# Choosing PSUM banks by a replay on another set of engine intervals, in an attention and feed-forward block

## The reference

```python
q = _rope(q, positions)
k = _rope(k, positions)
scores = jnp.einsum('bhqd,bhkd->bhqk', q, k) / jnp.sqrt(jnp.float32(dk))
scores = jnp.where(causal[None, None, :, :], scores, -jnp.inf)
attn = jax.nn.softmax(scores, axis=-1)
out = jnp.einsum('bhqk,bhkd->bhqd', attn, v)
...
x = _layernorm(x + _L0_attn_ref(x, L0_attn_W_qkv, L0_attn_W_o), axis=-1)
x = _layernorm(x + _L0_ffn_ref(x, L0_ffn_kernel, L0_ffn_bias, L0_ffn_a, L0_ffn_b), axis=-1)
```

## Time and profile before

| | |
|---|---|
| median of 3 runs | 437.37 us (437.16 to 437.58) |
| profiled execution | 437.25 us, span 435.5 us |
| busy, share of the span | PE 95%, PE weight loads 47%, DVE 86%, ACT 72%, POOL 26% |
| mean granted TensorE clock | 0.985 |
| chain that ended last | PE 78%, DVE 15%, ACT 4% |

### The profile page before, as it was taken

The page is one execution under the profiler, slowest core; times in us unless marked ns, Lnnn a source line. Parts: engine busy times, 40 slices in busy tenths (PEclk is TensorE's granted clock), DMA queues, the critical chain, the costliest instruction groups (busy, mean ns, idle before and its releaser), DMA issues.

```text
span 435.5 us, 8512 instructions
## 1 busy us (share of the span) xinstructions
PE 412.0 (95%) x3250; PEld 202.5 (47%) x3250; DVE 374.5 (86%) x487; ACT 313.5 (72%) x552; POOL 114.6 (26%) x184
## 2 busy tenths in 40 slices
PE   5999799999999999999999999999999999999992
PEld 2556444354335453465453544444354354436651
DVE  2878889999999989998899999999989977657586
ACT  2454765785776877686877797978786888898761
POOL 8879610202212111212011213003003001205534
PEclk9999889999999999999999999999999999999997
DMA  7522322200000000022200022200000000000011
GB/s 236 187 99 78 133 65 69 74 25 3 0 2 3 2 2 4 2 70 60 75 3 2 6 81 62 59 2 2 2 2 2 2 2 2 3 2 3 3 50 49
DMA packets 12200, 16.57 MB, mean 38 GB/s; under 512 B 2444, under 2 KB 7324, under 8 KB 12160
## 3 DMA queue, kind: packets, MB, share of 16 engines
q1 hardware_dynamic: 11072, 15.75, 11.6%
q0 software_dynamic: 1088, 0.28, 0.4%
HBM read 10.37 MB, written 5.24 MB: 36 GB/s over the span
## 4 chain that ended last, share of the span: by engine, by line
PE 78%; DVE 15%; ACT 4%; issue 2%; DMA 1%; SPq 0%; DVEq 0%; ACTq 0%
PE ps L1296 28%; PE ps L1280 19%; PE ps L1227 17%; DVE pmax L1038 13%; PE ps L1195 3%; ACT probs L961 3%; PE ps L1305 2%; PE ps L1241 2%; PE ps L1237 1%; PE ps L1211 1%; PE ps L1324 1%; PE ps L1201 1%; DMA x_sb<-in_L_attn_x_dram 1%; PE ps L1251 1%; PE ps L1328 1%
## 5 line engine op out<-in xcount | busy, mean ns | idle before, releaser
L1038 DVE TENSOR_REDUCE pmax<-ps 128x2 f32<-128x1024 f32 (+3 forms) x273 | 318.4, 1214 | 35.3 <-PE ps L1227 20.0
L961 ACT ACTIVATE probs<-ps 128x512 f32<-128x512 f32 (+4 forms) x485 | 282.1, 655 | 81.9 <-PE ps L1280 80.8
L1280 PE MATMUL ps<-qS,kS 64*128 64x512 f32 (+3 forms) x664 | 149.9, 404 | 2.8 <-DVE pmax L1038 2.3
L1296 PE MATMUL ps<-probs,vP 128*9 128x512 f32 (+3 forms) x1328 | 146.4, 520 | 0.2
L1227 PE MATMUL ps<-kS,qS 64*128 64x512 f32 (+3 forms) x640 | 137.1, 418 | 6.6 <-DVE pmax L1038 2.3
L1280 PEld LDWEIGHTS ps<-qS,kS 64*128 64x128 f32 x664 | 78.4, 187 | 81.0 <-ACT probs L961 45.6
L1227 PEld LDWEIGHTS ps<-kS,qS 64*128 64x128 f32 x640 | 64.9, 186 | 68.5 <-DVE pmax L1038 29.1
L868 POOL TENSOR_SCALAR_AFFINE_SELECT probs<-probs 128x512 f32<-128x512 f32 x64 | 40.4, 635 | 123.3 <-ACT probs L961 123.2
L877 POOL DMA_DIRECT2D qS<-mrows x34 | 19.6, 578 | 163.5 <-DVE mrows L1058 163.5
L1296 PEld LDWEIGHTS ps<-probs,vP 128*9 128x9 f32 x1328 | 21.1, 88 | 39.2 <-issue 26.8
L1241 PEld LDWEIGHTS ps<-causal_x,ident_x 64*128 64x128 f32 x188 | 17.9, 186 | 0.0
(11 more groups left out here) (120 smaller groups left out, 188.5 us busy)
## 6 DMA issues: line engine op xcount, KB each, us to landing
qS<-q_parts SPq DMA_DIRECT2D x52, 64.0 KB
kS<-k_parts SPq DMA_DIRECT2D x52, 64.0 KB
cs<-rope_tables_dram SPq DMA_DIRECT2D x4, 512.0 KB, 6.7
q_parts<-qp SPq DMA_DIRECT2D x4, 512.0 KB, 2.8
k_parts<-kp SPq DMA_DIRECT2D x4, 512.0 KB, 2.8
x_sb<-in_L_attn_x_dram SPq DMA_DIRECT2D x4, 256.0 KB, 5.8
out_dram<-rot SPq DMA_DIRECT2D x2, 256.0 KB, 2.4
qS<-mrows POOLq DMA_DIRECT2D x30, 8.0 KB, 1.8
```

Source lines behind the costliest of these rows:

```text
L961: nc.scalar.activation(probs[:, J % PRING, heads[0]:heads[-1] + 1:3 - len(banks), lo:hi], src, ACT.Exp, scale=float(DK) ** -0.5).then_inc( ...
L1038: nc.vector.tensor_reduce(dst, src, AX.X, ALU.max).then_inc(unit_free, 1)
L1280: last = nc.tensor.matmul(ps[:, bank, at:at + w], kS[rows, b, j // TPC, hp, (j % TPC) * TOK:(j % TPC + 1) * TOK], qS[rows, b, c, hp, lo:hi ...
L1296: last = nc.tensor.matmul(bank_of(("PV", n, 0))[VW * h:VW * h + VC, lo:hi], vP[:, j, HG * g + h, :], probs[:, J % PRING, h, lo:hi], start= ...
```

## The change

The change gives thirteen of the fifteen intervals of the replay other values. `TURNS` stays letter for letter, and so do all instructions and their order on PE, DVE, ACT and POOL. With the new intervals the model's banks come free at other times and in another order, so that `pair` and `single` take others: 708 of the 831 events that take banks hold other banks, and for 229 of them the holder that was released last, by the trace of the kernel before, is another event.

```diff
-    LOAD, COLUMN, GAP, ENTRY, EXIT = 0.096, 1 / 2400, 0.007, 0.122, 0.082
-    TO_ACT, TO_DVE, TO_PE, ACT_TO_PE = 0.302, 0.181, 0.149, 0.18
-    DVE_FIX, ACT_FIX, M_WORK, O_WORK, PLACED, VFIX = 0.064, 0.05, 0.51, 0.49, 1.25, 0.079
+    LOAD, COLUMN, GAP, ENTRY, EXIT = 0.1, 1 / 2400, 0.016, 0.115, 0.08
+    TO_ACT, TO_DVE, TO_PE, ACT_TO_PE = 0.29, 0.17, 0.13, 0.13
+    DVE_FIX, ACT_FIX, M_WORK, O_WORK, PLACED, VFIX = 0.155, 0.09, 0.6, 0.6, 1.25, 0.094
```

## The result

The first four runs of the changed kernel have a median of 447.35 us (445.45 to 449.76) against 437.39 us for the kernel before: a ratio of 1.0231, with a 95% interval from 1.0165 to 1.0297. Six more runs gave 448.64 us and 1.0247 (1.0205 to 1.0288). The runs don't scatter evenly. At a mean granted clock of 0.996 or 0.997 the changed banks took 445.21, 445.29, 445.45 and 445.47 us; the kernel before at 0.995 took 435.63, 435.95, 435.96 and 436.30 us. The means differ by 445.36 - 435.96 = 9.4 us. Over all 16 runs with the changed banks (three sets, one with the loads placed as before) the median is 449.3 us, 12 us above 437.4.

What follows compares the result with a forecast made beforehand. PE, busy 412.0 us (95%), was taken to bound the kernel. Terms 7.1 + 2.0 + 2.0 - 1.2 = +9.9 us on 437.25 gave 447.15, predicted as 447.3 us for the median; range 442.1 to 452.3 us.

Steps and rivals of the forecast that it cites:

- The mechanism: Attention part: instructions and busy time stay; PE waits longer where a bank now passes on from a later reader.
- the loads: SP's triggers: SP waits for units up to 5 places earlier, at 76 loads; taken as costing nothing.
- the named events: New waits at events starting at 136.75, 263.91, 319.67 and 384.46 us, each later by 0.6 to 1.3 us.
- The sum: Whole kernel: added waits less relief, +9.9 us on the profiled execution's 437.25 us.
- on the chain, no swap: 15 added waits where the chain runs through PE, no neighbour relieved, counted in full: 7.1 us.
- swaps on the chain: Nine chain waits (4.0 us) where the delayed event takes a bank a nearby later one waited for; half, 2.0 us.
- off the chain: Some 14 added waits where the chain runs through DVE or ACT; half of the 3.9 us without swaps, 2.0 us.
- relief: Chain waits shortened by earlier releases: 3.4 us stand alone, 1.06 at 362.97 us gives nothing, half the rest: -1.2 us.
- the second rival: Later PE waits absorb the added delays, leaving 437.4 us; chance 0.05.
- the matmul rows: At 362.97 us PV's matmuls fill the array until 363.04 us, so a set's earlier loads gain nothing of 1.06 us.
- The first rival: All banks: intervals nearer the trace give banks that are free sooner, 433.6 us; chance 0.05.
- The third: Past 105 us: longer waits bring two 60 us stretches to clock 0.94, 7 us more, 454.3 us; chance 0.04.

Runs made afterwards that it cites:

- the kernel without the wait at 57 us: Changed kernel with one event's bank moved, so the set at 57.04 us no longer inherits from the set just ahead: 446.53 us, ratio 1.0203.
- the fitted one: Kernel before with banks from a replay on intervals fitted to its trace's event starts, loads placed as before: 446.67 us, ratio 1.0190.
- the banks alone: Kernel before with banks from the new intervals and the loads' places from the old ones: 450.01 us, ratio 1.0266.

## Why the prediction was right

**The mechanism held.** Busy time grew by 1.1 us at most, the loads cost nothing that can be measured, and the waits appeared at the named events. The steps of the changed kernel's trace come to 9.0 us, and so do those of the kernel without the wait at 57 us, whose clock between 50 and 70 us is that of the kernel before (delay -0.16 us at 82 us, 8.86 at the end). The sum was 9.9 us. That it came so near is in part luck, since its errors go both ways:

**The terms, by the delay ahead of and behind each place in the changed kernel's trace:**

| term | predicted | measured |
|---|---|---|
| on the chain, no swap | 7.1 | 4.8 |
| swaps on the chain | 2.0 | 1.9 |
| off the chain | 2.0 | 2.5 |
| relief | -1.2 | -0.1 |

Which event a step is put down to moves up to some 0.5 us between the first three rows; their sum doesn't depend on it.

The swaps' half was right: at 352.74 us 0.99 us were added and the delay rose by 0.47. *The step that was too large* is that the unswapped waits count in full. Of 1.3 us at 384.46 some 1.15 stayed, of 0.65 at 136.75 and 0.67 at 273.0 0.6 each, of 0.87 at 319.67 0.6, of 0.46 at 269.22 0.3, and of 0.70 at 252.82 only 0.17. The price was counted from the event's weight load, which can run ahead of its matmul. The set priced at 384.46 us has its matmuls at 384.69 us before, and with the change at the time of its load, 392.15 us:

```profile
384.69 0.40 PE L1280 MATMUL ps<-qS,kS 64*128 64x512 f32 x2
...
392.15 0.50 PE L1280 MATMUL ps<-qS,kS 64*128 64x512 f32 x2 [0.87 <-ACT probs L961]
```

So 0.23 of the 1.3 us was no loss. At fourteen of the places on the chain, swaps included, such a lead of 0.11 to 0.24 us was used up, 2.9 us together, which can account for the error of 2.3 us. At 252.82 us the unit behind took back more: it had waited 0.43 us, and starts right behind now, so there the second rival was true in part.

```profile
253.54 0.22 PEld L1227 LDWEIGHTS ps<-kS,qS 64*128 64x128 f32 x2 [0.43 <-issue]
...
255.28 0.19 PEld L1227 LDWEIGHTS ps<-kS,qS 64*128 64x128 f32 x2
```

*Relief at half* was wrong the other way. At the place of the earlier trace rows the set still waits its 0.86 us and the array is full:

```profile
368.19 1.05 PE L1296 MATMUL ps<-probs,vP 128*9 128x512 f32 x8
...
369.17 0.52 PEld L1280 LDWEIGHTS ps<-qS,kS 64*128 64x128 f32 x5 [0.86 <-ACT probs L961]
```

The same holds at 238.65 us, where 0.44 us were to be had and the delay is level. So the matmul rows decided: at these places a full array was no headroom. The Trainium skill (Perfetto Trace Analysis, Identifying the Most-Contended Engine) says that matmul busy time is a bad measure of headroom; by that rule the term would have been -3.4 us, further from the -0.1 measured. *Off the chain* the half was too little at 263.91 us: DVE stood 0.68 us, as worked out (0.6), but the delay that stayed was 1.3 us.

**The first rival** (a replay nearer to the trace gives better banks) is refuted for a replay as near as the fitted one. **The third** was right that the clock falls too, and wrong in place and price: it was put behind 105 us, where the clock stayed at 1.00 up to 400 us in every profile, and the fall is the one that the kernel before already has near 50 us, made longer in some runs. It goes with some 2.5 us more in the median of 16 runs. Its reading of the earlier trace rows was off: the 1.1 us is of a wait ahead of 105 us, and from there to 400 us the longest of the 154 waits of units and sets for ACT and DVE is 0.9 us; the changed kernel has waits of up to 1.2 us there, at 1.00 as well. The predicted 447.3 us agrees with the first four runs' median because two of these runs were at a clock of 0.985 or less and two at 0.996 or more; the part that was argued is the 9.4 us at an equal clock, and the agreement to 0.1 us is luck.

## What to carry to other kernels

When a static assignment of buffers is derived by replaying a hand-written order on a model, order, model and assignment are one set: a more faithful model alone makes it slower, by 2% here, and so does 0.01 us in one constant. To price such a change, look up for each reassigned buffer when its new former holder's reader ends in the existing trace; count an added wait on the critical chain from the start of the event's matmuls and not of its weight load, half of it if a neighbour is relieved of the same release, and count relief as nothing where the engine is full. Compare variants at an equal granted clock. With the banks alone the stretch of low clock was some 13.6 us long in the profile, against 6.8 before (estimates from the PEclk of the windows above, at half clock), and one wait of under 1 us brought runs at 0.983 or less in four of twelve, where the kernel before has none.

## What the runs showed of the hardware that was not expected

The stretch at 1.2 GHz begins near 50 us, behind the prologue, and differs from run to run of one program: of the three profiles with all changed banks one has 1.00 from 50 us on, one a low clock far into 60 to 70 us, and one two short falls (0.83 in both windows). PE had been as busy ahead of it where the clock fell as where it didn't: 13.18 of the 15 us from 35 to 50 us in the kernel before, 13.23 in the changed kernel's profile. So what decides it stays open. A delay that stands at 66 us, 5.7 us between two of the profiles, is carried to the end unchanged, to 0.1 us over 370 us. Profiles also differ ahead of it, by up to 2.4 us at 20 us, where the kernels do the same.

That 774 of 831 events can move to other banks at no cost that can be measured (0.9988, with 1 inside the interval) says that a bank's number doesn't count here and the inheritance does. Whether neighbouring banks count was not tried; the reductions and exponentials take as long in the changed kernel as before (1216 ns for 1214, 655 for 655).
